# Another order for the first batch's preparation, with three low parts moved to GpSimd

## The reference

```
xn   = ln(x)
s    = sigmoid(silu(xn @ s_w1.T + s_b1) @ s_w2.T + s_b2)     # 256, then 128 wide
u    = (xn @ B_w.T + B_b) * s
h_t  = h_{t-1} @ A.T + u_t                                   # scan over the tokens
y    = hs @ C_w.T + C_b + xn @ D_w.T + D_b
x1   = x + ln(y * sigmoid(xn @ g_w.T + g_b))
x2   = ln(x1)
out  = x1 + ln(relu(x2 @ Ws1)**2 @ Ws2 + routed)
```

## Time and profile before

| what | us |
|---|---|
| median of three runs | 826.71 |
| lowest, highest run | 822.82, 884.32 |
| profiled execution, span from first to last instruction | 820.9 |
| PE busy in the span | 789.0 (96%) |
| DVE busy | 599.7 (73%) |
| POOL busy | 465.6 (57%) |
| ACT busy | 346.7 (42%) |

### The profile page before, as it was taken

The page is one execution under the profiler, slowest core; times in us unless marked ns, Lnnn a source line. Parts: engine busy times, 40 slices in busy tenths (PEclk is TensorE's granted clock), DMA queues, the critical chain, the costliest instruction groups (busy, mean ns, idle before and its releaser), DMA issues. The chain is left out here.

```text
span 820.9 us, 10797 instructions
## 1 busy us (share of the span) xinstructions
PE 789.0 (96%) x3644; PEld 650.4 (79%) x3644; DVE 599.7 (73%) x1393; ACT 346.7 (42%) x555; POOL 465.6 (57%) x560
## 2 busy tenths in 40 slices
PE   7989999999999999999999999999999999999985
PEld 6778878887888878888788887888788887888873
DVE  7858875697857977678775787578785797744774
ACT  4524435344433444344433544534443344432453
POOL 1243658438565576456574565844756557634555
PEclk9999999999999999999999999999999999999998
DMA  8524333544255424362334533354425522322112
GB/s 287 175 80 178 95 115 131 177 164 142 81 176 196 139 78 154 110 250 77 100 132 168 192 89 111 137 178 163 145 79 178 188 95 78 102 104 103 52 51 104
DMA packets 39614, 109.85 MB, mean 134 GB/s; under 512 B 6915, under 2 KB 23683, under 8 KB 31750
## 3 DMA queue, kind: packets, MB, share of 16 engines
q1 hardware_dynamic: 39126, 108.95, 39.4%
q10 hardware_dynamic: 432, 0.20, 0.1%
HBM read 60.84 MB, written 33.61 MB: 115 GB/s over the span
## 5 line engine op out<-in xcount | busy, mean ns | idle before, releaser
L1936 POOL TENSOR_TENSOR xres<-work,xres 128x512 f32<-128x512 f32 x64 | 83.1, 1299 | 65.1 <-DVE work L1324 65.1
L1896 POOL TENSOR_TENSOR rsv<-rsv,negh 128x1 f32<-128x1 f32 x64 | 53.3, 832 | 105.9 <-DVE rsv L1320 105.8
L495 PE MATMUL TM<-gw_hi,xT_hi 128*128 128x512 f32 x256 | 107.2, 419 | 0.0
L497 PE MATMUL TM<-gw_hi,xT_lo 128*128 128x512 f32 x256 | 100.7, 393 | 0.0
L497 PE MATMUL TM<-dw_hi,xT_lo 128*128 128x512 f32 x256 | 100.2, 391 | 0.0
L496 PE MATMUL TM<-gw_lo,xT_hi 128*128 128x512 f32 x256 | 100.1, 391 | 0.0
L495 PE MATMUL TM<-dw_hi,xT_hi 128*128 128x512 f32 x256 | 100.0, 391 | 0.0
L496 PE MATMUL TM<-dw_lo,xT_hi 128*128 128x512 f32 x256 | 99.6, 389 | 0.0
L987 ACT ACTIVATE work<-TM,nmz,rsz 128x512 f32<-128x512 f32 x62 | 48.2, 777 | 112.7 <-POOL nmz L1906 112.7
L1940 POOL TENSOR_TENSOR work<-work,xres 128x512 f32<-128x512 f32 x62 | 79.0, 1290 | 8.0 <-ACT work L987 8.0
L1246 DVE TENSOR_TENSOR xin<-xin,norm_row 128x1024 f32<-128x1024 f32 x56 | 71.2, 1305 | 11.4 <-ACT norm_row L932 11.4
(11 more groups left out here) (177 smaller groups left out, 2062.3 us busy)
## 6 DMA issues: line engine op xcount, KB each, us to landing
xres<-in_x SPq DMA_DIRECT2D x16, 1024.0 KB, 5.9
x_scratch<-xres SPq DMA_DIRECT2D x16, 1024.0 KB, 4.6
xin<-in_x SPq DMA_DIRECT2D x15, 1024.0 KB, 5.3
out<-work SPq DMA_DIRECT2D x30, 512.0 KB, 3.4
xin<-in_x_t SPq DMA_DIRECT2D x14, 1024.0 KB, 5.8
work<-x2q SPq DMA_DIRECT2D x112, 128.0 KB, 2.7
rows_in<-ln_scratch SPq DMA_DIRECT2D x14, 512.0 KB, 4.7
xin<-in_x SPq DMA_DIRECT2D x2, 512.0 KB, 5.1
```

The costliest lines, as they stand in the source:

```text
L495: eng.matmul(ps, lhs[0], rhs[0], start=first, stop=False)
L497: return eng.matmul(ps, lhs[1], rhs[0], start=False, stop=last)
L1896: return eng.tensor_tensor(dst, src, negh[:, 0:n], ALU.pow)
L1936: eng.tensor_tensor(xres[:, j, :], work[:, j, :], xres[:, j, :], ALU.add).then_inc(S["x1_ok"], 1)
```

## The change

Three things change, all for batch 0's preparation and the tail behind it. The low parts of s1, b and s2 go from DVE to POOL (DVE's list keeps g and d; POOL makes them ahead of and behind its power for tiles 4 to 7). The sums of the second half go to four other banks: H(1,0) to TM[2], H(1,1) to TM[0], B(1) to FM[1], SG(1) to FM[0]; so H's second half waits for no FM bank, B(1) waits for `s_gate(0)`, SG(1) for `u_of(0)`, and G(0,0) and G(0,2) wait for the `h1` that empties their banks. And the hand-written orders of PE, ACT, DVE and POOL are changed. Lines that only pass `rep` on to `fm_bank` are left out below.

```diff
-        LO_DVE = {n: i + 1 for i, n in enumerate(["s1", "b", "s2", "g", "d"])}
-        LO_POOL = {n: i + 1 for i, n in enumerate(["constants", "c", "f1", "f2"])}
+        LO_DVE = {n: i + 1 for i, n in enumerate(["g", "d"])}
+        LO_POOL = {n: i + 1 for i, n in enumerate(["constants", "s1", "b", "s2", "c", "f1", "f2"])}
...
-        def fm_bank(name):
-            return FM[slot(FM_RING, name)]
+        PREP_BANKS = {"h10": TM[2], "h11": TM[0], "b1": FM[1], "s1": FM[0]}
+
+        def fm_bank(name, rep=0):
+
+            return PREP_BANKS[name] if rep < 0 and name in PREP_BANKS else FM[slot(FM_RING, name)]
...
 def G(b, rep, j, steps={}):
                     weights("g")
+                if rep == 0 and j in (0, 2):
+                    eng.wait_ge(S["h1_ok"], prep_at("h1_ok", 0, 3 - j // 2))
...
 def H(b, rep, m, f):
-                wait_free(eng, FM_RING, name, b, rep, FM_FREED)
+                if not (rep < 0 and m):
+                    wait_free(eng, FM_RING, name, b, rep, FM_FREED)
...
 def B(b, rep, m):
-                wait_free(eng, FM_RING, f"b{m}", b, rep, FM_FREED)
+                if rep < 0 and m:
+                    eng.wait_ge(S["s_ok"], prep_at("s_ok", 0, 0))
+                else:
+                    wait_free(eng, FM_RING, f"b{m}", b, rep, FM_FREED)
...
 def SG(b, rep, m):
-                wait_free(eng, FM_RING, f"s{m}", b, rep, FM_FREED)
+                if rep < 0 and m:
+                    eng.wait_ge(S["u_ok"], prep_at("u_ok", 0, 0))
+                else:
+                    wait_free(eng, FM_RING, f"s{m}", b, rep, FM_FREED)
...
 PE, from L784
             power(3)
+            power(4)
             FT(-1, -1, 0)
-            power(4)
-            FT(-1, -1, 1)
             power(5)
             power(6)
+            FT(-1, -1, 1)
             power(7)
+            FT(-1, -1, 2)
             power(8)
-            FT(-1, -1, 2)
...
             power(12)
+            FT(-1, -1, 3)
             power(13)
-            FT(-1, -1, 3)
...
             power(17)
-            power(18)
-            power(19)
-            H(-1, -1, 0, 0)
             FT(-1, -1, 4)
             FT(-1, -1, 5)
+            H(-1, -1, 0, 0)
             FT(-1, -1, 6)
+            power(18)
             H(-1, -1, 0, 1)
+            FT(-1, -1, 7)
+            power(19)
             B(-1, -1, 0)
-            FT(-1, -1, 7)
             SG(-1, -1, 0)
-            power(20)
             H(-1, -1, 1, 0)
             H(-1, -1, 1, 1)
             B(-1, -1, 1)
             SG(-1, -1, 1)
+            power(20)
             first_tail(0, 0)
```

DVE's and POOL's orders:

```diff
 DVE, from L1770
             l1_ag(0, 2)
+            ln1_norm(0, 0)
             l1_ag(0, 3)
             l1_ep(0, 0)
-            ln1_norm(0, 0)
+            less_first_of("s1")
             ln1_norm(0, 1)
             ln1_norm(0, 2)
+            ft_low(-1, -1, 0)
             ln1_norm(0, 3)
-            less_first_of("s1")
-            ft_low(-1, -1, 0)
-            ft_low(-1, -1, 1)
             l1_bn(0, 4)
...
             l1_ag(0, 7)
+            less_first_of("b")
+            l1_ep(0, 1)
+            ft_low(-1, -1, 1)
             ft_low(-1, -1, 2)
-            l1_ep(0, 1)
-            low("s1")
-            ft_low(-1, -1, 3)
             ln1_norm(0, 4)
             ln1_norm(0, 5)
+            ft_low(-1, -1, 3)
             ln1_norm(0, 6)
+            ft_low(-1, -1, 4)
+            ln1_norm(0, 7)
             add_biases()
-            less_first_of("b")
             less_first_of("g")
-            low("b")
             h1(-1, -1, 0, 0)
-            ln1_norm(0, 7)
-            ft_low(-1, -1, 4)
+            ft_low(-1, -1, 5)
             h1(-1, -1, 0, 1)
-            low("s2")
-            ft_low(-1, -1, 5)
             ft_low(-1, -1, 6)
             ft_low(-1, -1, 7)
+            less_first_of("d")
+            low("g")
+            h1(-1, -1, 1, 0)
             u_of(-1, -1, 0)
-            low("g")
-            less_first_of("d")
-            h1(-1, -1, 1, 0)
             h1(-1, -1, 1, 1)
+            u_of(-1, -1, 1)
             low("d")
-            u_of(-1, -1, 1)
             first_tail(0, 0)
...
 POOL, from L2058
             pair_rs_of()
             ln1_rs(0, 0)
+            low("s1")
             ln1_rs(0, 1)
+            low("b")
+            low("s2")
             h1_low(0, 0, 0)
```

More of the change, by code:

```diff
@@ L647, in H @@
                     o = k * FH + f * P
-                    r = mm3(fm_bank(name)[:, :], [w[:, o:o + P] for w in s1_w],
+                    r = mm3(fm_bank(name, rep)[:, :], [w[:, o:o + P] for w in s1_w],
                             (xT_hi[:, js, k, :], xT_lo[:, js, k, :]), k == 0, k == KD - 1)
@@ L971, in sig @@
                 wait_free(eng, HF_RING, name, b, rep, HF_FREED)
-                eng.activation(hf_row(name), fm_bank(name)[:, :], ACT.Sigmoid, bias=b_col[:, f:f + 1])\
+                eng.activation(hf_row(name), fm_bank(name, rep)[:, :], ACT.Sigmoid, bias=b_col[:, f:f + 1])\
                    .then_inc(S["sig_ok"], 1)
@@ L981, in s_gate @@
                     eng.wait_ge(S["u_ok"], prep_at("u_ok", b + 1 if m else b, (m - 1) % NM))
-                eng.activation(sg[:, :], fm_bank(f"s{m}")[:, :], ACT.Sigmoid, bias=b_col[:, 2:3])\
+                eng.activation(sg[:, :], fm_bank(f"s{m}", rep)[:, :], ACT.Sigmoid, bias=b_col[:, 2:3])\
                    .then_inc(S["s_ok"], 1)
@@ L1132, in _ @@
             copy_power(9)
-            ft_hi(-1, -1, 2)
+            ft_hi(-1, -1, 1)
             copy_power(10)
@@ L1136, in _ @@
             copy_power(12)
+            ft_hi(-1, -1, 2)
             copy_power(13)
-            ft_hi(-1, -1, 3)
+            high_part("b")
             copy_power(14)
             copy_power(15)
+            ft_hi(-1, -1, 3)
+            ft_hi(-1, -1, 4)
             copy_power(16)
             copy_power(17)
[L1143 to L1146, removed]
             ft_hi(-1, -1, 5)
             high_part("s2")
-            copy_power(19)
+            sig(-1, -1, 0, 0)
+            ft_hi(-1, -1, 6)
             sig(-1, -1, 0, 1)
             high_part("g")
-            ft_hi(-1, -1, 6)
             ft_hi(-1, -1, 7)
+            sig(-1, -1, 1, 0)
             s_gate(-1, -1, 0)
-            sig(-1, -1, 1, 0)
+            copy_power(18)
             sig(-1, -1, 1, 1)
+            high_part("d")
+            copy_power(19)
+            s_gate(-1, -1, 1)
             copy_power(20)
-            high_part("d")
             high_part("c")
-            s_gate(-1, -1, 1)
             high_part("f1")
@@ L1363, in h1 @@
                 eng.wait_ge(S["sig_ok"], prep_at("sig_ok", b + 1, i))
-                eng.scalar_tensor_tensor(out=h, in0=fm_bank(name)[:, :], scalar=b_col[:, f:f + 1], in1=h,
+                eng.scalar_tensor_tensor(out=h, in0=fm_bank(name, rep)[:, :], scalar=b_col[:, f:f + 1], in1=h,
                                          op0=ALU.add, op1=ALU.mult).then_inc(S["h1_ok"], 1)
@@ L1380, in u_of @@
                 js = slice(m * MS, (m + 1) * MS)
-                eng.scalar_tensor_tensor(out=u[:, js, :].rearrange("p a b -> p (a b)"), in0=fm_bank(f"b{m}")[:, :],
+                eng.scalar_tensor_tensor(out=u[:, js, :].rearrange("p a b -> p (a b)"), in0=fm_bank(f"b{m}", rep)[:, :],
                                          scalar=b_col[:, 3:4], in1=sg[:, :], op0=ALU.add, op1=ALU.mult)\
@@ L1439, in first_tail @@
                 scan_add(*a, 0)
+                l1_bn(b + 1, 0)
                 scan_add(*a, 1)
-                l1_bn(b + 1, 0)
+                l1_bn(b + 1, 1)
                 scan_add(*a, 2)
+                l1_ag(b + 1, 0)
                 scan_add(*a, 3)
-                l1_bn(b + 1, 1)
+                l1_ag(b + 1, 1)
                 scan_add(*a, 4)
-                l1_ag(b + 1, 0)
                 scan_add(*a, 5)
-                l1_ag(b + 1, 1)
+                l1_bn(b + 1, 2)
                 scan_add(*a, 6)
-                l1_bn(b + 1, 2)
+                l1_bn(b + 1, 3)
                 scan_add(*a, 7)
-                l1_bn(b + 1, 3)
                 scan_add(*a, 8)
                 scan_add(*a, 9)
+                hs_low(*a, 0)
                 l1_ag(b + 1, 2)
+                l1_ag(b + 1, 3)
                 scan_add(*a, 10)
-                l1_ag(b + 1, 3)
                 l1_ep(b + 1, 0)
@@ L1461, in first_tail @@
                 scan_add(*a, 12)
+                scan_add(*a, 13)
+                l1_ag(b + 1, 4)
                 l1_bn(b + 1, 5)
-                scan_add(*a, 13)
                 l1_bn(b + 1, 6)
-                l1_ag(b + 1, 4)
-                scan_add(*a, 14)
-                hs_low(*a, 0)
                 l1_ag(b + 1, 5)
@@ L1471, in first_tail @@
                 l1_ag(b + 1, 7)
+                scan_add(*a, 14)
                 hs_low(*a, 1)
@@ L1770, in _ @@
             l1_bn(0, 0)
+            l1_bn(0, 1)
             l1_ag(0, 0)
-            l1_bn(0, 1)
             l1_ag(0, 1)
```

11 lines of the change are left out of this document (5 added, 6 removed).

## The result

The changed kernel takes **826.3 us** (median of 20 runs), the kernel before 823.4 in as many runs. The ratio, formed without the one slow run of 884.3 us, is 1.0025, with a 95% interval of 1.0014 to 1.0037. So the change makes the kernel slower, by 2.1 us by that ratio and by 2.9 by the two medians, where 2.1 us less were forecast; both are far inside 2%.

What follows compares the result with a forecast made beforehand. PE, busy 96%, bounds the kernel, so only its gaps can be won. Scan step 0 moves from 44.61 to 42.47, 2.14 less; span 820.9 to 818.8, plus 3.85 gives 822.6 us, range 820 to 825.5.

Steps and rivals of the forecast that it cites:

- Low parts on POOL: Batch 0's preparation: s1's low part takes 2.4 us on POOL, 12.7 to 15.1, at no cost; b and s2 nothing.
- Up to H(0,0): From batch 0's start to its first H sum: H(0,0) starts at 19.45, 0.15 later than before.
- rival 3: Batch 0's load of s1's first row lands late, H(0,0) 3.2 later: span 822.0, time 825.8; chance 0.10.
- PE leg: PE's queue up to H(0,0): power 17 ends near 18.5 as before, FT(4) and FT(5) follow to 19.35.
- POOL's power: POOL's power for tiles 4 to 7, before H(0,0): takes 1.01 instead of 1.91 without DVE's s1 part beside it.
- H(0,0) to scan 0: Batch 0 from 19.45: 21.2 to the end of SG(1) at 40.65, then 1.82 to scan step 0 at 42.47.
- two gaps: PE's stands before H(1,0), 1.44, which goes, and before the scan, 1.57; 0.45 goes between SG(1) and scan.
- Rival 1: Near the scan's start POOL's low part of c precedes DVE's of d, PE waits 0.7: time 823.3; chance 0.17.
- Rival 2: At PE's x2T wait at 107.36 the gain is given back, gap grows by 2.1: time 824.7; chance 0.15.
- Span to time: Around the span: 3.85 us, the middle of 1.9 and 5.8, added to span 818.8, giving 822.6.
- DVE's leg: DVE's chain before H(0,0): from 9.95 through norms and one `ft_low` to statistics of tiles 4 to 7 at 13.15.
- gate value: Between SG(1) and the scan, before the change: `sg` out of ACT at 43.23; DVE taking it at once saves 0.45.

Runs made afterwards that it cites:

- e1: Changed kernel with DVE's norm of tile 3 put ahead of the low part of tile 0's transpose; scan step 0 at 42.78, 4.16 earlier than in the changed kernel.
- e9: Changed kernel with norms 1 and 3 put earlier, POOL's b part waiting for norm 6, ACT's high part of b behind `ft_hi(3)`; 819.84 us, 0.36% under the kernel before.
- e3: Changed kernel with 36 matmuls of zeros in PE's two gaps, 24 before power 16 and 12 before FT(4); median 825.6 us.
- e4: Changed kernel with the low parts of s1, b and s2 back on DVE; median differs by 0.5 from the kernel before, ratio by nothing.
- e11: Changed kernel with only POOL's low part of b made to wait for the norm of tile 6; scan step 0 at 44.79, 2.15 ahead of the changed kernel.
- e10: The e9 kernel with the low parts of s1, b and s2 back on DVE; medians of the two differ by 1.0, scan step 0 at 42.48.
- e5: Kernel before with only the second half's sums in the four other banks and the waits these need; scan step 0 at 46.12.
- e8: Changed kernel run once more, unedited; its profiled execution took 822.96 us.
- e2: Changed kernel with ACT's high part of b put behind the copy of power 17; scan step 0 at 43.90, 3.04 earlier than in the changed kernel.
- e7: Changed kernel with norm 3 earlier, POOL's b part waiting for norm 6, ACT's high part of b behind power 17's copy; time falls by 0.3%.

## Why the prediction was wrong

*The step that failed* is "Low parts on POOL". It took 2.4 us for s1's part, from 12.7 to 15.1; measured 2.35 from 12.37. It then asked only whether DVE could hold POOL, found 1.4 us of cover, and took "no cost"; the parts of b and s2 it put at nothing in the same way. The other direction was not asked: what on DVE runs beside them. Norm 3 was issued 0.27 after s1's part and held (2.36 for 0.54), norm 4 just after b's (1.47). The Trainium skill, page "SBUF — State Buffer", section "Who interferes with whom", names `tensor_scalar` among the operations that can contend with GpSimd when their operands meet conditions, and says that the one issued first keeps the pair for its whole instruction. The trace agrees, 2.36 for 0.54. The prediction cites this section and says that the same lock stands over all that is moved to POOL; it priced it in both directions only for c and d, and for s1 only as time that POOL could lose.

*Up to H(0,0): 19.45 forecast, 22.65 measured.* `less_first_of("s1")` started at 9.97 (9.95 forecast), so rival 3's late load did not occur. The statistics started at 14.92 for 13.15, which is the hold; with norm 3 ahead they start at 13.21 (e1). The PE leg was put at 18.5 for the end of power 17 "as before"; it counted high b among ACT's copies as work of some 0.4, and did not follow its input back to DVE, for which it stood 1.89. POOL's power, taken at 1.01, took 1.01. The wait of FT(1) (1.22), which the sum doesn't have, was no part of the miss: with 0.86 of it left in e1, power 17 starts at 17.96, before at 18.08. It is a gain that the prediction did not see, and e9 takes it.

*H(0,0) to scan 0: 23.02 forecast, 24.29 measured.* With the clock at 1.00 it is 22.35 in e1 and 22.45 in e9, so the forecast was 0.6 to 0.7 too long. Powers 18 and 19 were put at 0.38 each, the duration shown; between other matmuls a power adds 0.14 (45.12 to 45.26 in the changed kernel), and this is 0.5 of it. What made the measured stretch longer all the same is the clock, which stood nowhere in the prediction. The miss at scan step 0 adds up: FT(4) late by 2.5 (21.06 for 18.53), the clock 2.5 (25.88 for e1's 23.41; e3 gives 2.7), less the 0.5 by which FT(4) to scan was taken too long (42.47 - 18.53 = 23.94, for e1's 23.41): 4.5 = 46.94 - 42.47.

*The two gaps* went as said: no wait before H(1,0), 0.73 before scan step 0 (under 1.0 was forecast), 1.82 from the end of SG(1) to it (45.12 to 46.94; 1.82 forecast). Rival 1 did not come: d's part went first (46.71, 2.28 long) and c's was held (3.38). Rival 2 did not either: the wait at 109.81 is 1.71 for 1.57, and that row moved by 2.45 as scan step 0 did by 2.33.

*Span to time.* 3.85 us were added for what lies around the span. The profiled executions of the study show 1.8 (827.15 for 825.4; 819.39 for 817.6), so 2.1 of the forecast's 822.6 were no part of the change; with 1.8 it would have been 820.6, 5.7 under what was measured instead of 3.7. So part of the nearness of the forecast is luck. Two smaller slips move nothing by more than 0.1: DVE's leg adds up to 13.20 and not 13.15, and the gate value's 43.23 is later used as 43.27.

*The rest of the span.* It grew by 4.5, scan step 0 by 2.33. In the changed kernel's execution the clock was at 0.86 in two windows behind waits for x2T (400 to 412 and 694 to 706), in that of before in the first alone; 0.14 of 12 us is 1.7. With that and 0.4 more of x2T waits the 4.5 is all there. The second window, before and changed:

```profile
694.00:706.00 12.00, 12.00 (x54) 9.93 (x53) 10.99 (x27) 4.95 (x8) 5.28 (x7) 1.00 0.19 45
```
```profile
694.00:706.00 12.00, 11.12 (x42) 9.03 (x43) 9.51 (x19) 4.59 (x8) 5.21 (x6) 0.86 0.15 34
```

*From scan step 0 to the time of all runs.* Medians follow scan step 0 of the one profiled execution only within about 2 us (e3 and e4 are the worst). Every run on record has its mean granted clock, and that explains most of it. In the 88 runs of the kernel before beside e1 to e11, 0.001 less of mean clock goes with 0.86 us more of time, and 0.4 us of scatter is left. The kernel before has a mean clock of 0.9937 over these runs, the changed kernel 0.9896 over its 20. At that rate the difference is worth 3.5 us, more than the 2.4 by which the two mean times (823.1 and 825.6) differ. Where both kernels have runs at the same mean clock, 0.992, the changed one is the faster: 823.8 (6 runs) for 824.8 (22 runs). So, by this estimate, what made it slower over all runs is the lower clock, and the rest of the change wins about 1 us. With span times mean clock as an estimate of the span without the lost clock, e9 is 3.5 us under the kernel before (scan step 0: 3.2), e10 2.4 (2.1) and e4 1.7 (2.0). The same estimate says that e3's zero matmuls gave back 2.3 us of clock, as expected, and that its runs lost 2.2 elsewhere, of which its profile shows the 0.85 of FT(4)'s later start. All this is worked out from sums over runs; no experiment isolates it.

What stays open: where in the other runs the clock fell. Only one execution of each kernel has a trace (two of the changed one), and the falls behind the x2T waits differ between them.

## What to carry to other kernels

When elementwise work moves from VectorE to GpSimd, look up what VectorE runs beside it in its new place: the question is who is issued first, in both directions, and a norm of 0.54 us issued a moment later pays the whole 2.35. Put statistics, or work with one input in PSUM, beside it, not a `tensor_scalar` on SBUF: in e1 three `bn_stats` beside the same part (there 12.49 to 14.92) took 1.88, as against 1.86 alone, and an `ft_low`, which reads PSUM, 0.69, as against 0.68. A stall of PE early in a kernel can cost nearly its length twice (here stands of 2.14 and 1.07, and 2.5 of clock), so follow every input of a queue (here ACT's high part) back to what it waits for, and read the granted clock behind each gap.

## What the runs showed of the hardware

- A `tensor_scalar` of 128x511 on SBUF is held by a GpSimd subtraction as a two-input operation is: 2.36 for 0.54 (norm 3), 1.47 (norm 4), each ending 0.28 to 0.29 after GpSimd's; and GpSimd's `h_lo` took 3.24 for 1.29 beside DVE's part of d (e5).
- In this stage the granted clock fell to 0.50 around PE's stands of 2.14 and 2.15 (changed, e8, and e11, where no long second stand followed), of 2.58 (e5) and of 1.10 and 1.27 (e2, e7), but not after 1.27 (e10), 1.21 (e4), 1.41 (e3) or 1.44 (before). So the length of one stand does not tell it. 36 small matmuls in the gaps kept it at 1.00 (e3).
- The run times of the kernel before lie in groups near 821.3, 823.0 and 824.7, at mean granted clocks of 0.996, 0.994 and 0.992. The step of 1.7 is what one fall behind a wait for x2T costs, and time and mean clock go together run by run; that the groups are a count of such falls is argued from the sizes, not shown.
